# Raw expert weights as the high operand: the split into high and low halves moves from ScalarE copies to VectorE ANDs

## Chip, cores and metric
The kernel runs on one core of a Trainium2 chip. The metric is the device time of one execution in microseconds. Time before: 564.48 us, the median of three runs (564.39 to 565.3).

## What is computed
One layer on 16 sequences of 256 tokens with 256 features: retention attention with 8 heads and a layer norm, then a mixture of 8 experts (each token goes to one of them) beside a shared feed-forward part, and a second layer norm. The experts are what the change touches. Cut to that:

```python
E, H, I = (8, 256, 512)
logits = x @ router_w.T
top_vals, top_idx = jax.lax.top_k(logits, 1)
scores = sigmoid(scatter(top_vals))                       # -inf elsewhere
xr = x[None, :, :] * scores.T[:, :, None]
gate_up = jnp.einsum('eth,ehf->etf', xr, gate_up_proj)    # [8, 256, 1024]
gate, up = jnp.split(gate_up, 2, axis=-1)
routed = jnp.einsum('etf,efh->eth', up * jax.nn.silu(gate), down_proj)   # [8, 512, 256]
shared = jax.nn.silu(x @ shared_gate_w) * (x @ shared_up_w) @ shared_down_w
x = layernorm(x + shared + routed.sum(axis=0))
```

## The kernel before
Five engines run one hand-written instruction list each; semaphores order them, and each list is worked through strictly in order. PE (the trace's name) is TensorE, DVE is VectorE, ACT is ScalarE, POOL is GpSimd, SP issues most DMAs.

**The main loop** runs t from 0 to 9 (PAIRS + 1). Step t projects the pair of sequences t, does attention of pair a = t - 1 and the shared feed-forward part and routing of pair f = t - 2. Step 8 has no projection any more, step 9 only the feed-forward part of pair 7. In the trace, step 3 is about 92.9 to 135.95 us, step 4 runs to 178.85, step 8 is 306.9 to about 347, step 9 ends at 365.15.

**The slots** follow. The tokens are sorted by expert into 39 slots of 128. For each slot GpSimd gathers the rows (`gather`), TensorE transposes them, multiplies by the gate and up weights of the slot's expert (`slot_gate_up`, matmuls on line 1657 through the helper `three`), transposes and multiplies by the down weights (`slot_down`, line 2036). The first three gathers stand before GpSimd's slot loop, gather(s + 3) at the head of turn s.

**High and low halves.** Products are made of three passes in a reduced 32-bit format (fp32r): high x high, high x low, low x high (`PASSES`). So every weight matrix exists as a high half (the value rounded to the format) and a low half (value minus high half). For the gate and up weights of the eight experts (128x2048 each) ScalarE makes the high half by a copy (`expert_hi`, L781) into `w_gu_hi`, in this order: expert 6 in step 3; 0 to 4 in step 8; 5 and 7 in step 9. The low half is a subtraction over the raw value in `w_gu`: on VectorE for seven experts (`expert_lo`, L1253), on GpSimd for expert 5 (`expert_rest`, L978). The places in each engine's list are written out by hand. Before slot 0 TensorE waits for all eight:

```python
pe.wait_ge(sig.ew_lo, EXPERTS - 1)
pe.wait_ge(sig.ew_lo2, 1)
```

For the down weights (128x1024 each) there is no room for both halves of all experts on chip. In steps 3 to 6 (`PARTED`, two experts a step) SP loads one into `dn_raw`, ScalarE copies it to `dn_top` (`down_top`, L789), GpSimd subtracts into `dn_low` (`down_rest`, L991), and SP stores both halves to scratch in device memory. Later all high halves are loaded into `w_dn` (three from step 7's list, one from step 9's, four by ScalarE's queue after the loop), and the low half of a slot's expert is loaded for each slot.

**Neighbours that the prediction speaks of.** On VectorE: `x_lo` (L1116), `variance` (L1170), `group_norm` (L1182), `gated` (the gating product, L1192), `shared_product` (L1208), `shared_sum` (L1223), `output_sum` (L1233), `go_on` (a copy of 8 columns, L1390), `rows_lo` (L1560). On GpSimd: `group_rstd` (var_e on L947 and two power instructions on L952, released by `variance`), `residual` (L958). `last_products` is VectorE's list of step 9: four shared products with expert subtractions between them, after which come shared_sum and rows_lo(0).

## Time and profile before
| | |
|---|---|
| runs | 564.48, 565.3, 564.39 us |
| span of the profiled execution | 562.4 us; the page gives no other time for it, the median of the runs is 2.08 us longer |
| busy in the span | TensorE 544.5 us (97%), VectorE 415.9 (74%), ScalarE 234.3 (42%), GpSimd 322.6 (57%) |
| mean granted TensorE clock | 0.996 of 2.4 GHz |
| DMA | 83.55 MB, 149 GB/s over the span |

The span runs from the first to the last instruction of the core. Busy times overlap between engines, and a share over the whole span averages stages with different limits; a timeline row gives start and length in microseconds, the instruction, its tiles (out<-in), how often it stands there, and in brackets the idle time of the engine before it with what ended it.

### The profile page before, as it was taken

To read this page: it belongs to the slowest core of one execution; us is meant where nothing else is said; L and a number is where in the kernel's file an instruction comes from. 1 tells how busy PE (TensorE), PEld (TensorE's weight loads), DVE (VectorE), ACT (ScalarE), POOL (GpSimd) and SP (SyncE) were. 2 spreads that over 40 slices of the span, in tenths; PEclk is the share of its full clock that TensorE was granted. 3 is DMA by queue.
4 is the path that set the end of the run, shared out by engine and by line. 5 is a ranking of instruction groups with operands and counts; after the bars stand their busy time and mean duration, and the time that the engine had idled before them with its cause. 6 is when DMAs were issued, how large, how long until landed. Compare 5 with 4: busy or idle time off the path is not lost.

```text
span 562.4 us, 11872 instructions
## 1 busy us (share of the span) xinstructions
PE 544.5 (97%) x3884; PEld 455.6 (81%) x3884; DVE 415.9 (74%) x866; ACT 234.3 (42%) x415; POOL 322.6 (57%) x320
## 2 busy tenths in 40 slices
PE   7998999999999999999999899999999999999994
PEld 5776788778779779779778578888888888888884
DVE  4888977878877877977966687747866666666664
ACT  3435342555453463363353765133333333333331
POOL 0535493496395396296294283715786556666544
PEclk9999999999999999999999999999999999999998
DMA  7901206507608507705375524666667666656651
GB/s 258 310 11 39 76 2 62 128 25 136 216 4 172 201 2 154 222 0 173 119 272 193 197 101 113 219 228 183 197 161 200 194 188 196 184 196 198 196 180 37
DMA packets 46505, 83.55 MB, mean 149 GB/s; under 512 B 11584, under 2 KB 30528, under 8 KB 46432
## 3 DMA queue, kind: packets, MB, share of 16 engines
q1 hardware_dynamic: 38736, 64.27, 37.9%
q0 software_dynamic: 6048, 15.39, 10.3%
q10 hardware_dynamic: 1664, 3.15, 1.5%
q8 instruction: 33, 0.54, 0.4%
q14 instruction: 24, 0.20, 0.1%
HBM read 60.85 MB, written 22.34 MB: 148 GB/s over the span
## 4 chain that ended last, share of the span: by engine, by line
PE 89%; DVE 3%; POOL 2%; issue 2%; ACT 1%; POOLq 0%; ACTq 0%; DVEq 0%
PE duo L1657 51%; PE duo L2036 9%; PE duo L1881 6%; PE duo L1713 5%; PE duo L1735 4%; PE duo L2046 3%; PE duo L1885 2%; PE duo L1871 1%; PE duo L1817 1%; PE duo L1925 1%; PE duo L1775 1%; PE duo L1861 1%; PE duo L1793 1%; DVE sims L1149 1%; PE duo L1842 0%
## 5 line engine op out<-in xcount | busy, mean ns | idle before, releaser
L1657 PE MATMUL duo<-w_gu_hi,xsT 128*128 x320 | 107.7, 399 | 0.0
L1657 PE MATMUL duo<-x1T,wsgu 128*128 128x512 f32 x384 | 93.2, 395 | 0.0
L1657 PEld LDWEIGHTS duo<-x1T,wsgu 128*128 128x128 f32 x384 | 71.0, 188 | 15.5
L935 POOL TENSOR_TENSOR turned<-turned,swapped 128x1024 f32<-128x1024 f32 x16 | 38.5, 2423 | 65.4 <-DVE swapped L1140 65.4
L1076 POOL DMA_INDIRECT out_rows<-of,seat x39 | 39.4, 1011 | 56.0 <-DVE of L1614 53.8
L1657 PEld LDWEIGHTS duo<-w_gu_hi,xsT 128*128 128x128 f32 x320 | 59.7, 188 | 11.3
L1657 PE MATMUL duo<-w_gu,xsT 128*128 x160 | 61.5, 384 | 0.0
L1569 DVE SCALAR_TENSOR_TENSOR eh<-duo,seat,e_act 128x512 f32<-128x512 f32 x38 | 28.6, 751 | 40.1 <-PE duo L1657 36.4
L1149 DVE TENSOR_TENSOR sims<-duo,causal 128x512 f32<-128x512 f32 x64 | 41.2, 686 | 15.8 <-ACT sims L682 15.8
L1067 POOL DMA_INDIRECT xz<-xz_d,seat x39 | 44.9, 1152 | 9.2 <-issue 9.0
L682 ACT ACTIVATE sims<-duo 128x256 f32<-128x256 f32 x64 | 21.1, 382 | 69.3 <-PE duo L1713 69.0
L952 POOL TENSOR_TENSOR rstd<-var_e,minus_half 128x16 f32<-128x16 f32 x16 | 46.5, 2920 | 0.7
L2036 PE MATMUL duo<-w_dn,ehT 128*128 x152 | 46.0, 302 | 0.0
L908 ACT ACTIVATE ehT<-duo 128x512 fp32r<-128x512 f32 x38 | 22.8, 600 | 54.5 <-PE duo L2046 31.0
L1015 POOL DMA_INDIRECT seat_d<-stage,place_i x32 | 35.4, 1107 | 13.2 <-issue 11.6
L2036 PE MATMUL duo<-w_dn,ehT_lo 128*128 x152 | 42.8, 282 | 0.0
L2036 PE MATMUL duo<-dn_rest,ehT 128*128 128x256 f32 x152 | 42.6, 280 | 0.0
L901 ACT ACTIVATE e_act<-duo,seat 128x512 f32<-128x512 f32 x38 | 26.2, 690 | 32.1 <-PE duo L1657 29.8
L1657 PE MATMUL duo<-xT,wqk 128*128 128x512 f32 x144 | 39.0, 409 | 0.1
L1713 PEld LDWEIGHTS duo<-turned 32*128 32x128 f32 x512 | 26.1, 184 | 13.0 <-issue 9.0
L1713 PE MATMUL duo<-turned 32*128 32x128 f32 (+1 forms) x512 | 34.0, 349 | 1.6 <-DVE sims L1149 1.6
L1881 PE MATMUL duo<-wsd_s,hT_hi 128*128 128x256 f32 x192 | 35.2, 285 | 0.0
(192 smaller groups left out, 1279.5 us busy)
## 6 DMA issues: line engine op xcount, KB each, us to landing
dn_rest<-dn_lo_d SPq DMA_DIRECT2D x39, 512.0 KB
w_gu<-L_ffn_gate_up_proj SPq DMA_DIRECT2D x8, 1024.0 KB, 7.4
x_in<-x_t SPq DMA_DIRECT2D x8, 512.0 KB
x_res<-L_attn_x SPq DMA_DIRECT2D x8, 512.0 KB, 4.2
xz_d<-zs SPq DMA_DIRECT2D x8, 512.0 KB
dn_raw<-L_ffn_down_proj SPq DMA_DIRECT2D x8, 512.0 KB
dn_hi_d<-dn_top SPq DMA_DIRECT2D x8, 512.0 KB, 3.5
dn_lo_d<-dn_low SPq DMA_DIRECT2D x8, 512.0 KB
```

The lines of the kernel that those rows point to most:

```text
L901: nc.scalar.activation(e_act[:, :], duo[s % 2][:, 0, :], ACT.Silu, scale=f32(seat[:, s, :])[:, 2:3])\
L935: nc.gpsimd.tensor_tensor(turned[:, g, :, :], turned[:, g, :, :], swapped[:, g, :, :], ALU.add)\
L952: nc.gpsimd.tensor_tensor(rstd[:, half], var_e[:, half], minus_half[:, half], ALU.pow)\
L1015: pool.indirect_dma_start(seat_d, bass.IndirectOffsetOnAxis(ap=place_i[:, q:q + 1], axis=0), stage[:, q, :], None).then_inc(sig.scat, 16)
L1067: pool.indirect_dma_start(xz[:, s % ROWS, :], None, known, bass.IndirectOffsetOnAxis(ap=seat[:, s, 0:1], axis=0))\
L1076: pool.indirect_dma_start(out, bass.IndirectOffsetOnAxis(ap=seat[:, s, 1:2], axis=0), of[:, s % OUTS, :], None).then_inc(sig.out_done[s % ...
L1149: nc.vector.tensor_tensor(sims[:, j % 4, :, 0::2, :], src, mask, ALU.mult).then_inc(sig.s_diag, 1)
L1569: nc.vector.scalar_tensor_tensor(out=eh[:, :], in0=duo[s % 2][:, 1, :], scalar=f32(seat[:, s, :])[:, 2:3], in1=e_act[:, :], op0=ALU.mult, ...
L1657: last = mm(out_, left(a, k), right(b, k), start=start and k == 0 and n == 0, stop=stop and k == kt - 1 and n == len(PASSES) - 1)
L1713: last = mm(sim_duo(a, j)[:, i % 2, SEQ * kb:SEQ * kb + SEQ - P * kb], turned[rows, g, 1, key:key + P], turned[rows, g, 0, key:SEQ * (b + 1)],
L1881: last = mm(duo[2][:, q // 2, D * (q % 2):D * (q % 2 + 1)], left[:, q * P:(q + 1) * P], wsd_s[:, b, n, :], start=n + m == 0, stop=n == FT ...
L2036: last = mm(duo[2][:, 1, 0:D], halves[left][:, f, :], weights[right], start=f + n == 0, stop=f == FT - 1 and n == len(PASSES) - 1)
```

## The change
The raw fp32 weight is itself given to TensorE as the high operand (its bits read as fp32r), so the high halves need no place of their own. `w_gu` stays raw and `w_gu_hi` becomes `w_gu_lo`. VectorE writes the weight with its lowest 12 bits cleared (an integer AND with -4096) into `w_gu_lo` (`expert_cut`), and a subtraction in place, raw minus cut, makes the low half there. VectorE subtracts for experts 6, 0, 3 and 7, GpSimd for 1, 2, 5 and 4; its first two subtractions stand before the gathers, the last two between gather(2) and the slot loop. The down weights go the same way in `dn_low` (`down_cut` on VectorE, `down_rest` on GpSimd); only low halves are stored, and `w_dn` is loaded straight from the input. ScalarE has no part in the split any more. The diff without most of its unchanged lines:

```diff
 ROUTE = 13
+TOP_BITS = -4096
 PASSES = ((0, 0), (0, 1), (1, 0))
...
         seat_d = scratch("seat_d", [SEATS, SEAT], I32)
-        dn_hi_d = scratch("dn_hi_d", [EXPERTS * P, FT * D])
         dn_lo_d = scratch("dn_lo_d", [EXPERTS * P, FT * D])
...
             dn_raw = p_sb("dn_raw", [P, FT * D])
-            dn_top = p_sb("dn_top", [P, FT * D], F32R)
             dn_low = p_sb("dn_low", [P, FT * D], F32R)
+            dn_spare = p_sb("dn_spare", [P, FT * D])
...
         sb = tensors(ctx)
-        w_dn = sb("w_dn", [P, EXPERTS, FT, D], F32R)
+        w_dn = sb("w_dn", [P, EXPERTS, FT, D])
         w_gu = sb("w_gu", [P, EXPERTS, KT, 2 * FF])
-        w_gu_hi = sb("w_gu_hi", [P, EXPERTS, KT, 2 * FF], F32R)
+        w_gu_lo = sb("w_gu_lo", [P, EXPERTS, KT, 2 * FF], F32R)
...
             dn_raw_in = new("dn_raw_in")
-            dn_top_ok = new("dn_top_ok")
+            dn_cut_ok = new("dn_cut_ok")
             dn_low_ok = new("dn_low_ok")
-            dn_top_out = new("dn_top_out")
             dn_low_out = new("dn_low_out")
...
             ehT_low_ok = new("ehT_low_ok")
-            ew_hi = new("ew_hi")
+            ew_cut = new("ew_cut")
             ew_lo = new("ew_lo")
...
-                    sp.wait_ge(sig.dn_top_out, 16 * EXPERTS)
                     sp.wait_ge(sig.dn_low_out, 16 * EXPERTS)
...
                 sp.wait_ge(sig.dn_low_ok, e + 1)
-                sp.dma_start(dn_hi_d[rows, :], f32(dn_top[:, :])).then_inc(sig.dn_top_out, 16)
                 sp.dma_start(dn_lo_d[rows, :], f32(dn_low[:, :])).then_inc(sig.dn_low_out, 16)
...
             def down_in(e):
-                sp.dma_start(f32(w_dn[:, e, :, :]).rearrange("p f d -> p (f d)"), dn_hi_d[P * e:P * (e + 1), :])\
-                    .then_inc(sig.edn_in, 16)
+                sp.dma_start(w_dn[:, e, :, :], down[e].rearrange("(k p) n -> p k n", p=P)).then_inc(sig.edn_in, 16)
...
                                          scale=ln_r[:, q:q + 1]).then_inc(sig.x1_ok, 1)
-            def expert_hi(e):
-                act.wait_ge(sig.egu_in[e], 16)
-                if e < 2:
-                    act.wait_ge(sig.g_ps, KT * PAIRS)
-                    act.wait_ge(sig.xT_lo, KT * PAIRS)
-                elif e < 4:
-                    act.wait_ge(sig.av_ps, 4 * PAIRS)
-                elif e == 4:
-                    act.wait_ge(sig.var_ok, 2 * PAIRS)
-                elif e == 5:
-                    act.wait_ge(sig.o_ps, 2 * PAIRS)
-                elif e == 7:
-                    act.wait_ge(sig.o_ps, 2 * (PAIRS - 1))
-                nc.scalar.activation(w_gu_hi[:, e, :, :], w_gu[:, e, :, :], ACT.Copy).then_inc(sig.ew_hi, 1)
-            def down_top(e):
-                act.wait_ge(sig.dn_raw_in, 16 * (e + 1))
-                if e:
-                    act.wait_ge(sig.dn_top_out, 16 * e)
-                    act.wait_ge(sig.dn_low_ok, e)
-                nc.scalar.activation(dn_top[:, :], dn_raw[:, :], ACT.Copy).then_inc(sig.dn_top_ok, 1)
...
                         squared(a)
-                    if t == PAIRS:
-                        expert_hi(0)
                 if has(t):
...
                     logits_copy(f)
-                    if t == PAIRS:
-                        expert_hi(1)
-                    if t == PAIRS + 1:
-                        expert_hi(5)
-                        expert_hi(7)
                 if has(t + 1) and t != 1:
...
                     h_high(f, 0)
-                    if t in PARTED:
-                        down_top(PARTED[t][0])
                     shared_act(f, 1)
...
                         y_scaled(a)
-                        expert_hi(2)
                     shared_act(f, 2)
                     h_high(f, 2)
-                    if t == PAIRS:
-                        expert_hi(3)
                     shared_act(f, 3)
                     h_high(f, 3)
-                    if t == PAIRS:
-                        expert_hi(4)
                 if has(a) and t < PAIRS:
...
                         y_top(a)
-                    if t == 3:
-                        expert_hi(EXPERTS - 2)
-                    if t in PARTED and len(PARTED[t]) > 1:
-                        down_top(PARTED[t][1])
                     if t == 1:
...
             act.wait_ge(sig.gu_ps, 2 * FT * PAIRS)
-            act.wait_ge(sig.dn_top_out, 16 * EXPERTS)
             for e in range(4):
-                act.dma_start(f32(w_dn[:, e, :, :]).rearrange("p f d -> p (f d)"), dn_hi_d[P * e:P * (e + 1), :])\
-                    .then_inc(sig.edn_in, 16)
+                act.dma_start(w_dn[:, e, :, :], k_rows(down[e])).then_inc(sig.edn_in, 16)
...
-                pool.wait_ge(sig.ew_hi, n)
-                nc.gpsimd.tensor_tensor(w_gu[:, e, :, :].bitcast(F32R), w_gu[:, e, :, :], f32(w_gu_hi[:, e, :, :]),
+                pool.wait_ge(sig.ew_cut, n)
+                nc.gpsimd.tensor_tensor(w_gu_lo[:, e, :, :], w_gu[:, e, :, :], f32(w_gu_lo[:, e, :, :]),
                                         ALU.subtract).then_inc(sig.ew_lo2, 1)
...
-                pool.wait_ge(sig.dn_top_ok, e + 1)
-                if e:
-                    pool.wait_ge(sig.dn_low_out, 16 * e)
-                nc.gpsimd.tensor_tensor(dn_low[:, :], dn_raw[:, :], f32(dn_top[:, :]), ALU.subtract)\
+                pool.wait_ge(sig.dn_cut_ok, e + 1)
+                nc.gpsimd.tensor_tensor(dn_low[:, :], dn_raw[:, :], f32(dn_low[:, :]), ALU.subtract)\
                     .then_inc(sig.dn_low_ok, 1)
...
-            pool.wait_ge(sig.plan_ok, 2)
-            expert_rest(5, EXPERTS - 1)
+            expert_rest(1, 3)
+            expert_rest(2, 4)
...
             gather(2)
+            expert_rest(5, 6)
+            expert_rest(4, 7)
             for s in range(SLOTS + 2):
...
+            def expert_cut(e):
+                dve.wait_ge(sig.egu_in[e], 16)
+                if e < 2:
+                    dve.wait_ge(sig.g_ps, KT * PAIRS)
+                    dve.wait_ge(sig.xT_lo, KT * PAIRS)
+                elif e < 4:
+                    dve.wait_ge(sig.av_ps, 4 * PAIRS)
+                elif e == 4:
+                    dve.wait_ge(sig.var_ok, 2 * PAIRS)
+                elif e == 5:
+                    dve.wait_ge(sig.o_ps, 2 * PAIRS)
+                elif e == 7:
+                    dve.wait_ge(sig.o_ps, 2 * (PAIRS - 1))
+                nc.vector.tensor_scalar(w_gu_lo[:, e, :, :].bitcast(I32), w_gu[:, e, :, :].bitcast(I32), TOP_BITS, None,
+                                        ALU.bitwise_and).then_inc(sig.ew_cut, 1)
             def expert_lo(e, n):
...
-                dve.wait_ge(sig.ew_hi, n)
-                nc.vector.tensor_tensor(w_gu[:, e, :, :].bitcast(F32R), w_gu[:, e, :, :], f32(w_gu_hi[:, e, :, :]),
+                dve.wait_ge(sig.ew_cut, n)
+                nc.vector.tensor_tensor(w_gu_lo[:, e, :, :], w_gu[:, e, :, :], f32(w_gu_lo[:, e, :, :]),
                                         ALU.subtract).then_inc(sig.ew_lo, 1)
+            def down_cut(e):
+                dve.wait_ge(sig.dn_raw_in, 16 * (e + 1))
+                if e:
+                    dve.wait_ge(sig.dn_low_out, 16 * e)
+                nc.vector.tensor_scalar(dn_low[:, :].bitcast(I32), dn_raw[:, :].bitcast(I32), TOP_BITS, None,
+                                        ALU.bitwise_and).then_inc(sig.dn_cut_ok, 1)
...
                 shared_product(f, 1)
+                expert_cut(3)
                 expert_lo(3, 5)
-                for j in range(2, FT):
-                    shared_product(f, j)
-                expert_lo(4, 6)
+                shared_product(f, 2)
+                expert_cut(5)
+                expert_cut(4)
+                shared_product(f, 3)
+                expert_cut(7)
                 expert_lo(7, 8)
...
                 elif t == PAIRS:
+                    expert_cut(0)
                     x1_lo(f)
...
                     variance(a)
+                if t in PARTED:
+                    down_cut(PARTED[t][0])
                 if has(t + 1):
...
                         dve.wait_ge(sig.nmr_ok, PAIRS)
-                        expert_lo(1, 3)
+                        expert_cut(1)
                 if t == 1:
...
                     if t == 3:
+                        expert_cut(EXPERTS - 2)
                         expert_lo(EXPERTS - 2, 1)
...
                         x1_lo(a)
+                    if t in PARTED and len(PARTED[t]) > 1:
+                        down_cut(PARTED[t][1])
                     if t <= PAIRS:
...
                     if t == PAIRS:
-                        expert_lo(2, 4)
+                        expert_cut(2)
                 if t == 1:
...
-            gu_flat = (w_gu_hi[:, :, :, :].rearrange("p e k n -> p (e k n)"),
-                       w_gu[:, :, :, :].rearrange("p e k n -> p (e k n)").bitcast(F32R))
+            gu_flat = (w_gu[:, :, :, :].rearrange("p e k n -> p (e k n)").bitcast(F32R),
+                       w_gu_lo[:, :, :, :].rearrange("p e k n -> p (e k n)"))
             halves = (ehT, ehT_lo)
-            dn_flat = w_dn[:, :, :, :].rearrange("p e f n -> p (e f n)")
+            dn_flat = w_dn[:, :, :, :].rearrange("p e f n -> p (e f n)").bitcast(F32R)
...
-            pe.wait_ge(sig.ew_lo, EXPERTS - 1)
-            pe.wait_ge(sig.ew_lo2, 1)
+            pe.wait_ge(sig.ew_lo, 4)
+            pe.wait_ge(sig.ew_lo2, 4)
             last_e = this_e = next_e = None
...
                 last_e, this_e = this_e, first_e if s == 0 else next_e

```

## Rows read from the trace of the kernel before
**Rows 1.** Busy time by stretch (us, busy, instructions; PEclk; DMA share, GB/s).
```profile
306.90:332.75 25.85, 22.71 (x204) 16.58 (x205) 19.45 (x43) 16.41 (x27) 12.42 (x12) 1.00 0.53 189
332.75:365.15 32.40, 32.40 (x153) 27.15 (x154) 24.31 (x41) 14.54 (x18) 19.21 (x14) 1.00 0.45 140
365.15:553.40 188.25, 187.63 (x1171) 166.16 (x1170) 123.99 (x301) 65.04 (x117) 109.72 (x152) 1.00 0.62 188
```

**Rows 2.** TensorE's timeline, steps 8 and 9 (start, length; idle before).
```profile
332.75 3.69 PE L1925 MATMUL duo<-wo,yT 128*128 128x256 f32 x16 [0.64 <-DVE yT L1192]
...
357.86 5.34 PE L1885 MATMUL duo<-wsd,hT 128*128 128x256 f32 x24
```

**Rows 3.** Groups by form, whole span (busy us, mean ns).
```profile
L1560 DVE TENSOR_TENSOR xsT<-duo,xsT 128x256 fp32r<-128x256 f32 x39 | 16.2, 416 | 0.3
L1614 DVE TENSOR_SCALAR of<-of,mv,ln_r 128x256 f32<-128x256 f32 x39 | 15.9, 407 | 1.0 <-POOL ln_r L1086 1.0
...
L781 ACT ACTIVATE w_gu_hi<-w_gu 128x2048 fp32r<-128x2048 f32 x8 | 15.2, 1907 | 0.0
```

**Rows 4.** VectorE's timeline, step 8.
```profile
318.43 1.29 DVE L1162 TENSOR_TENSOR x1T<-duo,x1T 128x512 fp32r<-128x512 f32 x2 [2.29 <-ACT x1T L707]
319.74 1.28 DVE L1170 TENSOR_REDUCE var<-retT 128x16 f32<-128x512 f32 x2
322.04 2.29 DVE L1253 TENSOR_TENSOR w_gu<-w_gu,w_gu_hi 128x2048 fp32r<-128x2048 f32 x1 [1.01 <-ACT w_gu_hi L781]
...
328.53 1.14 DVE L1390 COPY start<-start 128x8 f32<-128x8 f32 x1
```

**Rows 5.** GpSimd's timeline, step 8.
```profile
321.11 0.30 POOL L947 TENSOR_SCALAR var_e<-var 128x32 f32<-128x32 f32 x1 [8.20 <-DVE var L1170]
321.50 5.80 POOL L952 TENSOR_TENSOR rstd<-var_e,minus_half 128x16 f32<-128x16 f32 x2
327.26 2.38 POOL L958 TENSOR_TENSOR x_res<-x_res,bias_o 128x1024 f32<-128x1024 f32 x1
```

**Rows 6.** ScalarE's timeline, step 4.
```profile
174.17 1.06 ACT L789 ACTIVATE dn_top<-dn_raw 128x1024 fp32r<-128x1024 f32 x1 [1.32 <-DMA dn_raw<-L_ffn_down_proj]
```

**Rows 7.** VectorE's timeline before slot 0.
```profile
353.22 2.68 DVE L1253 TENSOR_TENSOR w_gu<-w_gu,w_gu_hi 128x2048 fp32r<-128x2048 f32 x1
...
358.67 4.48 DVE L1253 TENSOR_TENSOR w_gu<-w_gu,w_gu_hi 128x2048 fp32r<-128x2048 f32 x2
```

**Rows 8.** GpSimd's timeline before slot 0.
```profile
349.12 4.64 POOL L978 TENSOR_TENSOR w_gu<-w_gu,w_gu_hi 128x2048 fp32r<-128x2048 f32 x1 [8.91 <-ACT w_gu_hi L781]
353.91 2.94 POOL L1067 DMA_INDIRECT xz<-xz_d,seat  x1 [0.15 <-issue]
...
358.44 0.95 POOL L1067 DMA_INDIRECT xz<-xz_d,seat  x1 [0.31 <-issue]
359.69 2.07 POOL L1067 DMA_INDIRECT xz<-xz_d,seat  x1 [0.30 <-issue]
```

**Rows 9.** VectorE's timeline, steps 3 and 4.
```profile
131.72 2.29 DVE L1253 TENSOR_TENSOR w_gu<-w_gu,w_gu_hi 128x2048 fp32r<-128x2048 f32 x1 [1.11 <-issue]
...
135.12 1.28 DVE L1233 TENSOR_TENSOR x_res<-duo,x_res 128x512 f32<-128x512 f32 x2
...
157.92 1.29 DVE L1116 TENSOR_TENSOR xT<-x_in,xT 128x512 fp32r<-128x512 f32 x2 [1.60 <-ACT xT L664]
...
175.15 0.69 DVE L1223 TENSOR_TENSOR zs<-duo,x 128x512 f32<-128x512 f32 x1 [0.98 <-PE duo L1881]
```

**Rows 10.** TensorE's timeline at the start of step 4.
```profile
135.95 1.63 PE L1657 MATMUL duo<-xT,wqk 128*128 128x512 f32 x6
```

**Rows 11.** Busy time by stretch, after the last matmul.
```profile
555.40:557.90 2.50, 0.00 (x0) 0.00 (x0) 1.59 (x5) 0.00 (x0) 1.10 (x4) 1.00 0.00 0
558.00:562.40 4.40, 0.00 (x0) 0.00 (x0) 0.07 (x1) 0.00 (x0) 1.75 (x2) 0.50 0.17 60
```

**Rows 12.** TensorE's timeline, opening.
```profile
1.46 5.02 PE L1938 MATMUL duo<-y 128*128 128x256 f32 x14 [1.46 <-DVE y L1413]
```

## Prediction
> **What bounds the kernel now.** I read the page's totals first (the table above): TensorE 97% busy, ScalarE 42%. An average says nothing about a stage, so next came the table by stretch [rows 1]. The reader is to see that TensorE works through all of 332.75 to 365.15 and 187.6 of the 188.3 us of the 39 slots, and that there is one stretch where it really idles: step 8, 306.9 to 332.75, with 22.71 of 25.85 us busy. So whatever makes TensorE start later after 332.75 is on the end in full, and a lighter ScalarE pays only if it closes part of those 3.1 us of idling. Third, TensorE's own timeline [rows 2]: the last wait before the slots is 0.64 us at 332.75, put down to VectorE's gating product; the last shared down projection begins at 357.86, and slot 0 follows it without a pause at 365.15. There is thus one gate to watch: the wait for all eight low halves in front of slot 0. Fourth come groups by form for the prices, and last the timelines of VectorE and GpSimd in step 8, before slot 0 and in steps 3 and 4, to see who is late.
>
> **What is removed.** ScalarE loses eight expert copies of 1.907 us, 15.3 us in all [rows 3], and eight of the down weights, half as large. It loses them beside TensorE work. The only visible idle of step 8 behind which ScalarE could stand is the 0.64 us at 332.75. That wait ends with the gating product on VectorE, which comes after go_on's tiny copy, and the copy lasts from 328.53 to 329.67 although it moves 8 elements: it ends with GpSimd's residual add (327.26 + 2.38 = 329.64) [rows 4, 5]. That residual comes after the two power instructions of 321.5 to 327.3, so step 8 hangs on GpSimd and the gain is 0 (bounds 0 and 0.64). Eight stores of 512 KB also go, and the eight loads of w_dn now come from the input in 1 KB pieces; no engine waits for them before slot 0's down projection, some 7 us after the gate. I cost them at nothing; without that cover the nearest row is ScalarE's wait of 1.32 us for a load of the same shape [rows 6].
>
> **Price of the AND.** No row shows a 128x2048 AND. Upper bound: VectorE's subtraction of that size, 2.29 us when nothing disturbs it [rows 4], and by the slope between it and the 128x256 form (0.416) 1.22 us for 128x1024. Lower bound: the same slope halved over a base of 0.16 us, 1.22 and 0.69 us, an estimate. I take the lower: the tensor-scalar instruction on 128x256, with two scalars read per partition, takes 0.407 us, less than the 0.416 of a subtraction of that size without any [rows 3]; at one element at a time the two scalars should cost something.
>
> The Trainium skill ("VectorE: DVE Perf Modes", the perf-mode tier table) gives an fp32 tensor-scalar of 2048 elements in SBUF 1.227 us; by it the sum stays as below, by the upper bound it becomes rival B.
>
> **What two engines do to each other.** At 353.22 a VectorE subtraction with two SBUF inputs takes 2.68 us instead of 2.29: GpSimd's subtraction was running until 353.76. The gather that GpSimd issues at 353.91 then takes 2.94 us and ends 0.95 us after VectorE is done at 355.90. The one at 359.69 takes 2.07 us and ends 0.85 us after the first of VectorE's two subtractions, which began at 358.67 [rows 7, 8]. The tiny copy above waited for GpSimd in the same way. I read this as: these VectorE instructions and GpSimd's exclude each other for a whole instruction, and who waits goes next when the other ends.
>
> The Trainium skill ("SBUF — State Buffer", who interferes with whom) says so: the shared port pair is an exclusive lock, taken by two-port VectorE instructions and, against GpSimd's reads, by those with two SBUF inputs. The trace agrees (2.68 against 2.29 us). By that rule the AND itself locks; without it the sum is rival A's.
>
> **Steps 3 to 6, down weights.** The first AND of a step stands behind the variance and ahead of x_lo, where VectorE idles 1.60 us in step 4 [rows 9]: 0.69 us is hidden. It may hold GpSimd's var_e back by half a microsecond; the chain behind that has about as much slack, so 0 (at most 0.1 us in each of four steps). The second stands between the two halves of shared_sum, where VectorE idles 0.98 us in step 4: 0 too; ScalarE waited for the load there until 174.17, and VectorE comes for it at that time [rows 6, 9]. In step 3 there is no such idle. There the expert's AND (130.6 to 131.8) just replaces the 1.11 us of idling in front of the subtraction at 131.72; but the down AND (0.69, less the 0.08 by which VectorE's instructions overlap) pushes output_sum by 0.61 us. Its first half ends at 136.42 instead of 135.81, and TensorE, whose next projection started at 135.95 right behind it, starts it **0.6 us** later [rows 9, 10]. At the upper price it is 1.0 + 1.1 = 2.1 us.
>
> **Step 8.** cut(0) falls into the 2.29 us that VectorE idles before x1_lo at 318.43. That has a consequence: expert 0's subtraction no longer waits for ScalarE until 322.04, but follows the variance, which ends at 321.02, at once [rows 4]. GpSimd's var_e, released by that variance, came at 321.11 [rows 5]. Now VectorE is first by about 0.1 us and holds the lock until 320.94 + 2.29 = 323.2; the power instructions, residual add, go_on, find_seats and gating product all move by 2.1 us. TensorE's output projection starts at 334.8 instead of 332.75: **+2.05 us** (bounds 0, if var_e wins, and 2.1). All later local times below are shifted by this, which I leave out of them.
>
> **The gate of slot 0.** GpSimd: before, one subtraction (4.64 us) [rows 8]; now four. rest(1) and rest(2) follow ANDs that stand where VectorE's subtractions 1 and 2 stood; I take them to end about when the one subtraction ended, 353.8, so that gathers 0 to 2 fill the gaps up to 359.3, as before. VectorE: cut(3) starts at 353.22, where lo(3) did [rows 7]; 1.22 for it, 2.29 for lo(3), 0.69 for product(2) and 1.22 for cut(5), less the overlaps, end at 358.4, cut(4) at 359.55, product(3) at 360.15; TensorE needs it after the first twelve matmuls of the down projection, 357.86 + 2.7 [rows 2], so in time. GpSimd gets the lock at 359.6 and keeps it through rest(5) to 364.2. Only then cut(7) runs, to 365.4; rest(4) has waited and goes next, to 370.0; lo(7) ends at 372.3, shared_sum 372.9, rows_lo(0) 373.3. Were lo(7) to go ahead of rest(4), rest(4) would end at 372.35. So slot 0's matmuls start at 372.35 to 373.3 instead of 365.15: **+7.2 to 8.15, I take 7.7 us**. Behind this wait stands all of the slot work of TensorE. gather(3), now behind both subtractions on GpSimd, is needed only two slots later.
>
> **The clock.** The granted clock is 1.00, that is 2.4 GHz, in the slots [rows 1]; after the last matmul, from 555.4 on, the clock still reads 1.00 until 557.9 and then 0.50, that is 1.2 GHz [rows 11]: an idle of 7 to 8 us is long enough for it to fall. What a restart costs is bounded by 0 and by slot 0's twelve gate-up matmuls (2.8 us) at half speed. Nearest row: the 14 opening matmuls took 5.02 us [rows 12], where 24 of the same form take 5.34 [rows 2], that is 3.1 for 14. I take the difference, rounded up, **2.0 us**. The Trainium skill ("TensorE: Matmul & The Clock Gate", the HAM clock gate) has an idle array fall to 1.2 GHz and start again from there; no row in the middle of this trace shows it.
>
> **Sum.** 0.6 + 2.05 + 7.7 + 2.0 = 12.35 us on a span of 562.4, so 574.75. The runs' median is 564.48, 2.08 us above the span; that stays around it: **576.8 us**, 2.2% slower. A change under 0.2% (1.1 us) cannot be told from none.
>
> **Rivals.**
> *A, no exclusion of that kind.* Then var_e is not held (0), and rest(5) and rest(4) run back to back from 358.6 to 368.0: +2.85, an idle too short to be sure of a slower clock. With 0.6: +3.45, 567.9 us. For it: GpSimd's power instructions ran beside VectorE's subtraction at 322.04, and the gather of 358.44 beside that of 358.67, without harm [rows 4, 5, 7, 8]; against it the rows of 2.68, 2.94 and 1.14 us [rows 4, 7, 8]. Chance 0.12.
> *B, the AND goes one element at a time.* Then it takes 2.29 us and VectorE is late: 2.1 in step 3, 2.05, product(3) at 363.2 (TensorE needs it at 360.6), slot 0 at 373.2: 2.1 + 2.05 + 8.05 + 2.0 = 14.2, 578.7 us. For it: no large two-at-a-time instruction in the trace; against it the 0.407 us row [rows 3]. Chance 0.13.
> *C, not slower.* The four GpSimd subtractions vanish beside TensorE, as the one did, and ScalarE's relief closes step 8's waits. It decides if rest(4) is done by 365.15. The AND of expert 5 cannot end before 358.4, so each of the two subtractions would have to take 3.35 us instead of 4.64. Then 562.4 - 0.64 + 0.6 is 562.4, that is 564.4 us, no change; if all 3.1 us of idling went, 562.0, faster. Chance 0.05 (0.02 of it faster).
> The forecast keeps 0.70. **Range** 570 to 580 us: it leaves out A and C and holds the forecast without clock loss (574.8), without step 8's loss (574.8), without both (572.7), and B with the full 2.8 us. Faster 0.02, same 0.03, slower 0.95.
>
> **What the next profile would show.** TensorE idle 7 to 8 us before the first matmul that reads w_gu, its PEclk under 1 just behind; four GpSimd subtractions of 4.6 us or more, the last ending after 370 (plus the shift); VectorE ANDs of 1.2 us, the one of expert 7 stretched to some 5; var_e of step 8 about 2 us late; step 3 longer by half a microsecond, steps 4 to 6 unchanged; ScalarE under 219 us and none the faster for it. I am wrong if GpSimd's subtractions run freely beside VectorE's (A), if the ANDs take 2.3 us (B), or if TensorE does not wait at the gate (C).

## The result and the profile after
The changed kernel takes 579.35 us (median of 4 runs, 578.92 to 579.54) beside 564.43 for the kernel before: ratio 1.0264, 95% interval 1.0253 to 1.0276, slower by 14.9 us. The forecast was 576.8 us, range 570 to 580. The profiled run took 579.54 us, its span is 577.6 (562.4 before). Line numbers are the changed kernel's own: L1215 `expert_cut`, L1221 and L930 the subtractions on VectorE and GpSimd, L1229 `down_cut`.

The page's totals and granted clock show the direction: TensorE was at 97% before, ScalarE at 42%; now it is 95% and 37%, and slice 27 of 40 (14.4 us each) has a lower clock.

```profile
PE 548.9 (95%) x3884; PEld 457.2 (79%) x3884; DVE 434.1 (75%) x879; ACT 212.6 (37%) x399; POOL 340.4 (59%) x323
...
PEclk9999999999999999999999999979999999999998
```

TensorE's timeline (start, length, idle before) says where. The marks to compare are the first projection after each of steps 3 to 6 (135.95, 178.78, 221.75, 264.72 before), the output projection of step 8 (332.75 in [rows 2]) and the start of slot 0 (365.15 in [rows 1]). The kernel before, with the last shared matmuls and slot 1's first:

```profile
178.78 1.66 PE L1657 MATMUL duo<-xT,wqk 128*128 128x512 f32 x6
...
221.75 1.66 PE L1657 MATMUL duo<-xT,wqk 128*128 128x512 f32 x6
...
264.72 1.66 PE L1657 MATMUL duo<-xT,wqk 128*128 128x512 f32 x6
...
363.25 1.89 PE L1885 MATMUL duo<-wsd,hT 128*128 128x256 f32 x8
...
369.16 0.50 PE L1657 MATMUL duo<-w_gu_hi,xsT 128*128 x1
```

The changed kernel:

```profile
137.19 1.63 PE L1642 MATMUL duo<-xT,wqk 128*128 128x512 f32 x6 [1.04 <-DVE x_res L1184]
...
180.21 1.66 PE L1642 MATMUL duo<-xT,wqk 128*128 128x512 f32 x6
...
223.42 1.66 PE L1642 MATMUL duo<-xT,wqk 128*128 128x512 f32 x6
...
266.64 1.66 PE L1642 MATMUL duo<-xT,wqk 128*128 128x512 f32 x6
...
336.63 3.69 PE L1910 MATMUL duo<-wo,yT 128*128 128x256 f32 x16 [0.82 <-DVE yT L1143]
...
367.22 1.89 PE L1870 MATMUL duo<-wsd,hT 128*128 128x256 f32 x8
377.37 0.79 PE L1642 MATMUL duo<-w_gu,xsT 128*128 x1 [8.26 <-DVE xsT L1545]
...
384.30 0.49 PE L1642 MATMUL duo<-w_gu,xsT 128*128 x1
```

The delay grows by 1.24 us in step 3, by 0.19, 0.24 and 0.25 in steps 4 to 6, by 1.96 up to the output projection, and the last shared matmul ends 3.97 us late (369.11 instead of 365.14). Then TensorE idles 8.26 us, where before it did not idle. From slot 0's first matmul to slot 1's first it then takes 6.93 us (377.37 to 384.30); in the run with a busy TensorE below that is 4.27, so 2.66 are lost. Sum: 1.24 + 0.68 + 1.96 + 0.09 + 8.26 + 2.66 = 14.9 of the 15.2 us that the span grew. The 0.3 that is missing is slot 0's first matmul, which before began at 364.80, ahead of the last shared one's end. Slot 1 begins 15.14 us late (384.30 instead of 369.16), so the slots behind it lose next to nothing.

The table by stretch shows the last term: PEclk falls while TensorE idles (0.55 from 373 to 375) and reads 0.50 in slot 0's matmuls.

```profile
371.00:373.00 2.00, 0.00 (x0) 0.00 (x0) 2.00 (x1) 0.00 (x0) 1.84 (x2) 1.00 0.55 176
373.00:375.00 2.00, 0.00 (x0) 0.00 (x0) 1.97 (x2) 0.00 (x0) 1.70 (x1) 0.55 0.00 1
...
381.00:383.00 2.00, 2.00 (x7) 1.39 (x5) 0.11 (x1) 0.02 (x1) 0.00 (x0) 0.50 0.71 242
383.00:385.00 2.00, 1.58 (x9) 1.04 (x8) 1.07 (x2) 0.98 (x2) 0.00 (x0) 0.89 0.07 7
```

VectorE's timeline, in the places of [rows 4, 7, 9], has the causes.

```profile
130.91 1.29 DVE L1215 TENSOR_SCALAR w_gu_lo<-w_gu 128x2048 int32<-128x2048 int32 x1
132.23 2.29 DVE L1221 TENSOR_TENSOR w_gu_lo<-w_gu,w_gu_lo 128x2048 fp32r<-128x2048 f32 x1
...
135.04 0.81 DVE L1229 TENSOR_SCALAR dn_low<-dn_raw 128x1024 int32<-128x1024 int32 x1
...
136.36 1.27 DVE L1184 TENSOR_TENSOR x_res<-duo,x_res 128x512 f32<-128x512 f32 x2
...
322.86 2.28 DVE L1221 TENSOR_TENSOR w_gu_lo<-w_gu,w_gu_lo 128x2048 fp32r<-128x2048 f32 x1
...
364.17 9.69 DVE L1215 TENSOR_SCALAR w_gu_lo<-w_gu 128x2048 int32<-128x2048 int32 x1
373.89 2.29 DVE L1221 TENSOR_TENSOR w_gu_lo<-w_gu,w_gu_lo 128x2048 fp32r<-128x2048 f32 x1
376.10 0.68 DVE L1174 TENSOR_TENSOR zs<-duo,x_last 128x512 f32<-128x512 f32 x1
376.70 0.41 DVE L1545 TENSOR_TENSOR xsT<-duo,xsT 128x256 fp32r<-128x256 f32 x1
```

And GpSimd's, beside [rows 5, 8]: var_e of step 3 and of step 8, then the subtractions of experts 5 and 4 back to back.

```profile
113.45 0.67 POOL L899 TENSOR_SCALAR var_e<-var 128x32 f32<-128x32 f32 x1 [0.81 <-DVE var L1121]
...
323.04 2.27 POOL L899 TENSOR_SCALAR var_e<-var 128x32 f32<-128x32 f32 x1 [8.21 <-DVE var L1121]
...
363.79 8.97 POOL L930 TENSOR_TENSOR w_gu_lo<-w_gu,w_gu_lo 128x2048 fp32r<-128x2048 f32 x2
```

The reader is to see the long AND of expert 7: an instruction of 1.2 us elsewhere takes 9.69 because it waits until both GpSimd subtractions (to 372.76) are through. After it come lo(7), a shared sum and the rows of slot 0, and only these release TensorE at 377.37.

### The profile page after: what moved, and what is told of

It reads as the page before. It is cut to its first block, busy times and chain, and to the rows that moved or that the text cites. A ratio compares the mean times of both kernels' runs of the same rounds, so it can differ in the third digit from the quotient of the medians.

```text
span 577.6 us, 11854 instructions
## 1 busy us (share of the span) xinstructions
PE 548.9 (95%) x3884; PEld 457.2 (79%) x3884; DVE 434.1 (75%) x879; ACT 212.6 (37%) x399; POOL 340.4 (59%) x323
## 4 chain that ended last, share of the span: by engine, by line
PE 75%; issue 8%; DVE 8%; POOL 6%; ACT 1%; POOLq 0%; DVEq 0%; ACTq 0%
PE duo L1642 44%; PE duo L2021 9%; PE duo L1866 4%; PE duo L1698 4%; PE duo L1720 3%; PE duo L2031 3%; DVE w_gu_lo L1215 2%; PE duo L1856 1%; POOL turned L887 1%; PE duo L1910 1%; PE duo L1870 1%; POOL rstd L904 1%; PE duo L1802 1%; PE duo L1760 1%; POOL seat_d L965 1%
## 5 line engine op out<-in xcount | busy, mean ns | idle before, releaser
L1642 PE MATMUL duo<-w_gu,xsT 128*128 x320 | 109.4, 405 | 8.3 <-DVE xsT L1545 8.3
L1642 PEld LDWEIGHTS duo<-w_gu,xsT 128*128 128x128 f32 x320 | 60.8, 191 | 20.5 <-issue 8.8
L1642 PE MATMUL duo<-w_gu_lo,xsT 128*128 x160 | 62.4, 390 | 0.0
```

What stands on the lines that cost most here:

```text
L1642: last = mm(out_, left(a, k), right(b, k), start=start and k == 0 and n == 0, stop=stop and k == kt - 1 and n == len(PASSES) - 1)
```

## Experiments
All runs are of the changed kernel with one edit, unless it says otherwise; ratios are to the kernel before, with 95% intervals.

**The gate: two subtractions taken from GpSimd.**
```diff
-            expert_rest(5, 6)
-            expert_rest(4, 7)
...
                 expert_cut(7)
+                expert_lo(5, 6)
+                expert_lo(4, 7)
                 expert_lo(7, 8)
...
-            pe.wait_ge(sig.ew_lo, 4)
-            pe.wait_ge(sig.ew_lo2, 4)
+            pe.wait_ge(sig.ew_lo, 6)
+            pe.wait_ge(sig.ew_lo2, 2)
```


> The changed kernel with the subtractions of experts 5 and 4 on VectorE instead of GpSimd. Mine (the gate of slot 0 is set by GpSimd's two subtractions, 8.97 us, through which VectorE's AND of expert 7 waits): VectorE then does AND 7 and three subtractions from 364.2, ends at 372.1, and TensorE starts slot 0 at about 373.1 with 4.0 us of idle instead of 8.26: 575.1 us, and down to 572.4 if the idle is too short for the clock to fall. The AND of expert 7 takes 1.24 us instead of 9.69. Rival one (the gate waits for the loads of experts 5, 4 and 7 and not for an engine): idle stays at 8 us, 579.3. Rival two (rival A of the prediction, engines do not exclude each other, the long AND is a wait for data): the AND stays long, 579.

574.98 us, ratio 1.0182 (1.0161 to 1.0202): 4.4 us back. VectorE's and TensorE's timelines of this run:

```profile
363.87 1.21 DVE L1213 TENSOR_SCALAR w_gu_lo<-w_gu 128x2048 int32<-128x2048 int32 x1
365.00 6.68 DVE L1219 TENSOR_TENSOR w_gu_lo<-w_gu,w_gu_lo 128x2048 fp32r<-128x2048 f32 x3
```
```profile
372.87 0.79 PE L1642 MATMUL duo<-w_gu,xsT 128*128 x1 [4.06 <-DVE xsT L1545]
...
379.65 0.50 PE L1642 MATMUL duo<-w_gu,xsT 128*128 x1
```
The AND is 1.21 us, the idle 4.06: the gate is the engines' time, not the loads. The clock still fell in these 4 us: slot 0 takes 6.78 us from first matmul to first matmul, so that term stays, 2.5 us.

**The clock: needless matmuls in the wait.**
```diff
+            for n in range(60):
+                mm(duo[0][:, 0, 0:P], ident[:, :], ident[:, :], start=True, stop=True)
             pe.wait_ge(sig.ew_lo, 4)
```


> The changed kernel with 60 needless 128x128 matmuls of ident in the wait ahead of slot 0, into a bank that slot 0 overwrites. Mine (the 2.7 us that slot 0's first twelve matmuls lose are the clock, which fell in the idle): the gate stays at 377.4, PEclk reads 1.00 throughout, the twelve matmuls take 2.8 us instead of 5.5: 576.65 us. Rival (they are slow because they share the memory with the loads and gathers that run at that time): they still take 5.5 us, 579.35.

581.93 us, ratio 1.0308 (1.029 to 1.0326), slower than expected: each of the 60 ran as two, they lasted 13.56 us and outlasted the gate by 4.7. The twelve matmuls behind them nevertheless ran at full speed: 4.25 us from slot 0's first matmul to slot 1's. So again with 32:

> As the run with 60 needless matmuls, with 32: each of them ran as two, so 60 lasted 13.56 us and outlasted the gate by 4.7 us; 32 last 7.2 us and end some 1.3 us before it. Clock theory: the gate at 377.3, the twelve matmuls 2.8 us, 576.65 us. Rival (contention with loads, of which there are fewer at 382 than at 377): the twelve matmuls take 5.5 us again, 579.35.

576.58 us, ratio 1.0219 (1.0205 to 1.0233): 2.8 us back. TensorE's timeline and the table by stretch:

```profile
368.64 7.31 PE L2083 MATMUL duo<-ident 128*128 128x128 f32 x64
377.09 0.49 PE L1642 MATMUL duo<-w_gu,xsT 128*128 x1 [1.14 <-DVE xsT L1545]
...
381.36 0.49 PE L1642 MATMUL duo<-w_gu,xsT 128*128 x1
```
```profile
377.00:380.00 3.00, 2.91 (x13) 2.37 (x14) 0.44 (x1) 0.69 (x1) 0.00 (x0) 1.00 0.75 233
```
The gate is where it was, the DMA share is no lower (0.75, and 0.68 in the same stretch of the changed kernel), and slot 0 takes 4.27 us at PEclk 1.00. The last term was the clock, not contention.

**Step 8: who begins first.** Three runs change only what stands between the variance and expert 0's subtraction: a wait for var_e; that wait and four one-column memsets; that wait and one reduction. The edit of the third, where `c_in` counts four early loads, that of `bias_o` among them:
```diff
                     variance(a)
+                    dve.wait_ge(sig.eps_ok, a + 1)
+                    dve.wait_ge(sig.c_in, 16 * 4)
+                    nc.vector.tensor_reduce(pace[:, 0:2], bias_o[:, :].rearrange("p (a b) -> p a b", a=2), X, ALU.add)
                     expert_lo(0, 2)
```


> The changed kernel with expert 0's subtraction on VectorE made to wait until GpSimd's var_e of step 8 is written. Mine (step 8 lost 1.95 us because the subtraction got ahead of var_e and held it for 2.27 us): var_e takes 0.3 us and all of step 8 behind it comes 1.9 us earlier, 577.4 us. Rival (the subtraction then runs into the power instructions or delays the group norm, so the loss moves): var_e short, but the output projection no earlier, 579.3.

579.0 us, ratio 1.0261 (1.0238 to 1.0285): nothing back. My theory fell: var_e is short now, but the power instructions take the loss over. GpSimd's timeline, with the subtraction beginning at 323.23:

```profile
322.89 0.30 POOL L899 TENSOR_SCALAR var_e<-var 128x32 f32<-128x32 f32 x1 [8.20 <-DVE var L1121]
323.27 7.90 POOL L904 TENSOR_TENSOR rstd<-var_e,minus_half 128x16 f32<-128x16 f32 x2
```


> As the run in which expert 0's subtraction waits for var_e, with four one-column memsets on VectorE between that wait and the subtraction. There the subtraction began at 323.23 and the two power instructions, due 0.04 us later, took 7.90 us instead of 5.80. Theory now (GpSimd's power instruction waits for a VectorE subtraction that has begun, but runs beside one that begins later): the power instructions begin first and take 5.8 us, the output projection comes 1.9 us earlier, 577.4 us. Rival (the power instructions are slowed by any subtraction beside them, or the loss moves to y): 579.0 as without the memsets.

579.18 us, ratio 1.0262 (1.0248 to 1.0276), and 7.93 us: the memsets took no time of their own, so this run told nothing new.

> As the run in which expert 0's subtraction waits for var_e, with one reduction over bias_o (one input in SBUF, some 0.3 us) between. The four memsets had put no time between (subtraction 322.96, power instructions 322.97, 7.93 us). Theory: with the power instruction begun first it is not held; the two take 5.8 us and the output projection comes 1.9 us earlier, 577.4 us. Rival one (any subtraction beside a power instruction holds it for its 2.1 us, whichever began first): still 7.9 us, 579.2. Rival two (the loss moves to y or to the subtraction's place on VectorE): 5.8 us, but 579.

577.02 us, ratio 1.0224 (1.021 to 1.0238): 2.3 us back. GpSimd, VectorE and TensorE in this run:

```profile
323.24 5.80 POOL L905 TENSOR_TENSOR rstd<-var_e,minus_half 128x16 f32<-128x16 f32 x2
```
```profile
323.53 2.28 DVE L1222 TENSOR_TENSOR w_gu_lo<-w_gu,w_gu_lo 128x2048 fp32r<-128x2048 f32 x1
```
```profile
334.50 3.69 PE L1914 MATMUL duo<-wo,yT 128*128 128x256 f32 x16 [0.69 <-DVE yT L1144]
```
The same two instructions side by side, but the power instruction began 0.29 us earlier: 5.80 us, and the output projection is at 334.50 instead of 336.63. Beginning 0.04 us later had cost it 2.1.

**The down weights alone undone.** ScalarE's `down_top`, `dn_top`, the stores of the high halves and the reloads come back as in the kernel before; `down_cut` goes.
```diff
+                nc.scalar.activation(dn_top[:, :], dn_raw[:, :], ACT.Copy).then_inc(sig.dn_top_ok, 1)
...
-                nc.vector.tensor_scalar(dn_low[:, :].bitcast(I32), dn_raw[:, :].bitcast(I32), TOP_BITS, None,
-                                        ALU.bitwise_and).then_inc(sig.dn_cut_ok, 1)
```


> The changed kernel with the down weights split as before (copy on ScalarE, both halves stored, w_dn loaded from the stored high halves), the gate-up weights as changed. Mine (the two ANDs of a step cost 1.1 us in step 3, of which 0.39 by holding var_e back, and 0.2 us in each of steps 4 to 6): 1.8 us comes back, 577.55 us, the projection of step 4 starts 0.1 us after that of the kernel before instead of 1.24. Rival one (step 3 lost its time to the AND of expert 6): about 0.6 us comes back, 578.7. Rival two (the stores and loads of the high halves that return cost as much as the ANDs): 579.3.

577.16 us, ratio 1.0222 (1.0204 to 1.0239): 2.2 us back. TensorE's projections behind steps 3 and 6 stand at or ahead of their places before (135.95 and 264.72):

```profile
135.85 1.62 PE L1651 MATMUL duo<-xT,wqk 128*128 128x512 f32 x6 [0.20 <-DVE x_res L1205]
...
264.51 1.66 PE L1651 MATMUL duo<-xT,wqk 128*128 128x512 f32 x6
```
The AND of expert 6, still in step 3, leaves 0.2 us of idle; the rest was the down weights' ANDs. At step 6's mark the run is 2.13 us ahead of the changed kernel (264.51 instead of 266.64), nearly all that came back.

**The raw operand alone.** The kernel before, with the raw weights as the high operand and the low half written over ScalarE's copy; the edit is the same in both subtractions.
```diff
-                nc.vector.tensor_tensor(w_gu[:, e, :, :].bitcast(F32R), w_gu[:, e, :, :], f32(w_gu_hi[:, e, :, :]),
+                nc.vector.tensor_tensor(w_gu_hi[:, e, :, :], w_gu[:, e, :, :], f32(w_gu_hi[:, e, :, :]),
...
-            gu_flat = (w_gu_hi[:, :, :, :].rearrange("p e k n -> p (e k n)"),
-                       w_gu[:, :, :, :].rearrange("p e k n -> p (e k n)").bitcast(F32R))
+            gu_flat = (w_gu[:, :, :, :].rearrange("p e k n -> p (e k n)").bitcast(F32R),
+                       w_gu_hi[:, :, :, :].rearrange("p e k n -> p (e k n)"))
```


> The kernel before with one part of the change alone: TensorE reads the raw gate-up weights as the high operand, and the subtraction writes over ScalarE's copy, in place. The copies stay on ScalarE, the subtractions where they were. Mine (the operand itself costs nothing; all of the loss comes from who makes the halves and when): 564.4 us, within 0.2%. Rival (raw operands or in-place subtraction cost time in the slots): each 1% on the 39 slots' 187 us gives 1.9 us, 566 or more.

564.1 us, ratio 1.0 (0.9991 to 1.0009; 11 runs). The operand and the subtraction in place cost nothing that 11 runs can tell.

**The order at the gate.** One run, no interval.
```diff
             expert_rest(5, 6)
+            gather(3)
             expert_rest(4, 7)
             for s in range(SLOTS + 2):
-                if is_slot(s + 3):
+                if s and is_slot(s + 3):
                     gather(s + 3)
```


> The changed kernel with GpSimd's fourth gather between its subtractions of experts 5 and 4 instead of behind both. Mine (locks add up, whatever their order): VectorE's AND of expert 7 gets in behind the first subtraction and takes 5.5 us instead of 9.69, but the last of the chain ends no earlier: the first matmul of slot 0 at 377 to 378, span 577 to 578.5. Rival (the order costs it: had the AND gone in between, as the prediction had it, lo(7) would overlap the second subtraction's wait): gate 1 to 2 us earlier.

578.72 us, span 576.0. VectorE, GpSimd and TensorE:

```profile
363.84 5.24 DVE L1216 TENSOR_SCALAR w_gu_lo<-w_gu 128x2048 int32<-128x2048 int32 x1
369.11 2.29 DVE L1222 TENSOR_TENSOR w_gu_lo<-w_gu,w_gu_lo 128x2048 fp32r<-128x2048 f32 x1
```
```profile
363.46 4.52 POOL L930 TENSOR_TENSOR w_gu_lo<-w_gu,w_gu_lo 128x2048 fp32r<-128x2048 f32 x1
368.14 1.78 POOL L1016 DMA_INDIRECT xz<-xz_d,seat  x1 [0.16 <-issue]
369.94 5.83 POOL L930 TENSOR_TENSOR w_gu_lo<-w_gu,w_gu_lo 128x2048 fp32r<-128x2048 f32 x1
```
```profile
375.97 0.79 PE L1643 MATMUL duo<-w_gu,xsT 128*128 x1 [7.20 <-POOL w_gu_lo L930]
```
Mine was right on the AND (5.24 us) and wrong on the gate: slot 0 begins at 375.97 and the idle is 7.20 instead of 8.26, as the rival had it. The locked times do add up in either order, but now GpSimd is the last, and the sum and slot 0's rows (0.9 us) run beside its subtraction instead of behind it.

**The same work, placed anew.** Three runs. The first moves expert 6 to step 7 (its subtraction to GpSimd), puts the first down AND of a step and expert 0's subtraction behind var_e and four memsets, ANDs 1 to 3 into step 8, and leaves GpSimd only experts 6 and 1.

> The changed kernel with the same work placed by what the other runs showed: expert 6's AND in step 7 and its subtraction on GpSimd behind that step's seats; the first down AND of a step and expert 0's subtraction behind var_e and four small memsets; ANDs 1, 2 and 3 in step 8; only experts 6 and 1 subtracted on GpSimd, the rest on VectorE. Mine: steps 3 to 6 give back 2.0 us, step 8 gives back 1.9, the gate's idle falls from 8.26 to between 0 and 1 us and the clock does not fall (2.7): 564.4 to 565.5 us, the time before, not under it. Rival (VectorE has no room for 6 ANDs and 5 subtractions there): the gate keeps 2 to 3 us, 567 to 568, or 570 with the clock.

571.38 us, ratio 1.0119 (1.0104 to 1.0134). Steps 3 to 6 are back at their old places and the gate is gone: TensorE goes from the shared projection into slot 0 at 372.16 without idling. But the power instructions are held as before (7.93), and there is a new wait. VectorE, GpSimd and TensorE:

```profile
343.04 4.39 DVE L1275 CAST slots_f<-slots_i 128x8 f32<-128x8 int32 x1
```
```profile
342.84 4.55 POOL L931 TENSOR_TENSOR w_gu_lo<-w_gu,w_gu_lo 128x2048 fp32r<-128x2048 f32 x1
```
```profile
351.14 1.89 PE L1810 MATMUL duo<-x1T,wr 128*16 128x512 f32 x4 [2.96 <-DVE x1T L1113]
```
A cast of 8 columns, 0.17 us elsewhere, takes 4.39 because it waits for GpSimd, and behind it wait x1_lo and TensorE. The clock fell twice on the way: after waits of 0.33 and 1.22 us in step 8 twelve matmuls took 4.21 us (3.00 in the changed kernel), and after the 2.96 us PEclk read 0.50 from 351 to 353.

> The run with the work placed anew, mended where its profile showed two waits (power instructions of step 8 7.93 us; the plan's one 8-element cast 4.39 us, because GpSimd's subtraction of expert 1 ran, and so x1_lo 3 us late): expert 0's AND ahead of the last masked similarities and its subtraction on GpSimd ahead of var_e, expert 1's subtraction on GpSimd only when the plan is made, go_on's copy ahead of GpSimd's residual add. Mine: 2 us back in step 8, 3 us behind it, 0.6 from go_on's copy: 564 to 566 us, the time before within 0.3%. Rival (what TensorE no longer waits for there, VectorE then lacks at the gate): 567 to 569.

569.07 us, ratio 1.0084 (1.007 to 1.0097), short of mine: I had put the AND of expert 1 where GpSimd's subtraction of expert 0 runs, 4.58 us with x1_lo behind it (2.9 us of TensorE), AND 2 beside a power instruction of the seats and AND 3 beside one of the last norm. GpSimd, where AND 2 runs from 334.82 to 336.04:

```profile
333.81 2.27 POOL L958 TENSOR_TENSOR stage<-powed,minus_one 128x4 f32<-128x4 f32 x1
```

It takes 1.04 us in the changed kernel. Begun 1.01 us ahead of the AND, it still ended with it; so did the norm's (342.46 to 344.47, AND 3 from 343.21 to 344.43).

> The last placing with its two new waits mended. There expert 1's AND waited 3.4 us for GpSimd's subtraction of expert 0 with x1_lo behind it (2.9 us of TensorE), and the ANDs of experts 2 and 3 held GpSimd's one-column power instructions, so that the last norm came 1.2 us late. Now ANDs 1 and 3 stand behind the variance and a small reduction, where VectorE waits for TensorE, AND 2 behind the plan and the norm's scales, and GpSimd's subtraction of expert 1 behind AND 2. Mine (TensorE then waits 0.4 us in step 8 and 0.2 to 0.7 at the gate more than in the kernel before): 564.4 to 565.5 us, the time before within 0.2%. Rival (VectorE is full from step 8 to the gate, and any place for these ANDs delays something): 567 or more.

The edit is against the run before it; the first line puts GpSimd's subtraction of expert 1 behind AND 2.
```diff
-            expert_rest(1, 3)
+            expert_rest(1, 5)
...
-                    expert_cut(1)
                     x1_lo(f)
                     variance(a)
+                    dve.wait_ge(sig.eps_ok, a + 1)
+                    dve.wait_ge(sig.c_in, 16 * 4)
+                    nc.vector.tensor_reduce(pace[:, 0:2], bias_o[:, :].rearrange("p (a b) -> p a b", a=2), X, ALU.add)
+                    expert_cut(1)
+                    expert_cut(3)
...
-                        expert_cut(2)
...
                         plan_early()
-                        expert_cut(3)
+                        dve.wait_ge(sig.nmr_ok, PAIRS)
+                        expert_cut(2)
...
-                        expert_lo(2, 4)
-                        expert_lo(3, 5)
+                        expert_lo(2, 5)
+                        expert_lo(3, 4)
```
564.9 us (11 runs), ratio 1.0017 (1.0007 to 1.0026): the whole split without ScalarE, 14.5 us faster than the changed kernel and within 0.3% of the kernel before. TensorE's waits (total, times, longest) and its timeline at the gate:

```profile
PE duo L1735 <- DVE sims L1103: 2.1, 2, 1.2
```
```profile
360.54 2.86 PE L1885 MATMUL duo<-wsd,hT 128*128 128x256 f32 x12 [0.29 <-DVE hT L1162]
...
365.26 0.49 PE L1657 MATMUL duo<-w_gu,xsT 128*128 x1
```
No gate is left (slot 0 starts at 365.26 without a wait); the similarities wait 2.1 us in all (1.7 before), because expert 0's AND stands in front of the last, and 0.29 us go ahead of the last shared projection.

## Why the prediction was right, and where its terms were off
The direction, the order of the terms and most of the mechanism held; the forecast was 2.6 us too low, and the time is near the upper end of the range. Errors did not cancel: every term that was off by more than 0.1 us was too low.

- **Removed work, 0.** Held as far as the runs tell. Without ScalarE's copies TensorE still waits for the gating product in step 8, 0.82 us (0.64 before). The raw operand with the copies takes 564.1 us, the last placing without them 564.9. No run takes away ScalarE's work and nothing else, so the 0 itself is not shown. The stores and reloads that went are worth little: with them back the run was faster by 2.2 us, for the ANDs that went.
- **Price of the AND, 1.22 and 0.69 us.** Held: 1.21 to 1.29 and 0.68 where nothing disturbs it. Rival B is out.
- **Step 3, 0.6 us.** The mechanism was right and half of it was missing: 1.24. The down AND delays output_sum by 0.73, 0.12 of them because it is that much longer than elsewhere (0.81 us, while GpSimd's store of the seats runs); expert 6's AND is 0.12 slower than the idle that it fills; and the first down AND holds var_e (0.67 instead of 0.30), which arrives at y_rest as 0.39 (129.63 instead of 129.24).
- **Steps 4 to 6, 0.** A step that failed: "the chain behind that has about as much slack, so 0 (at most 0.1 us in each of four steps)". It was 0.19, 0.24 and 0.25. Holding var_e back was seen (its median is 0.67 us instead of 0.30), the slack behind it overrated; the run without down ANDs has none of the loss.
- **Step 8, 2.05 us.** It was 1.96, by the mechanism named: the subtraction is first by 0.18 us and var_e waits. What I had not seen is that the power instruction behind var_e can be held just so; in the kernel before it had begun 0.54 us ahead of the subtraction [rows 4, 5]. The "for it" of rival A (power instructions ran beside the subtraction without harm) thus told only who came first. The Trainium skill ("SBUF — State Buffer", who interferes with whom) says that the order of issue decides who blocks; the pair of runs with 7.90 and 5.80 us agrees. The two power instructions of the second placing that began ahead of an AND and still ended with it do not.
- **The gate, 7.7 us.** It was 8.26, just above the term's upper bound of 8.15. The step "who waits goes next when the other ends" failed for the AND of expert 7, which was to be stretched to some 5 us and took 9.69: GpSimd's second subtraction followed the first at once, and the AND, lo(7), the sum and the rows came behind both. The size came out near all the same, because with lo(7) last the engines' times add up alike in either order; the 7.7 was a middle between lo(7) last and the second subtraction last. With a gather between, the AND went in after the first subtraction, lo(7) followed it while GpSimd was at the gather, and the idle was 7.20, the lower bound of the term.
- **The clock, 2.0 us.** It was 2.66, near the upper bound: all of slot 0's gate-up matmuls ran at 0.50, that is 1.2 GHz. The Trainium skill ("TensorE: Matmul & The Clock Gate", the HAM clock gate) has an idle array fall to that clock; the run with a busy TensorE, at 1.00 throughout, agrees.
- **Rivals.** A is out by the instructions that waited (9.69, 4.39 and 7.90 us). C is out for this placing; the last run shows that it was a matter of placing.

## What to carry to other kernels
When work moves from ScalarE to VectorE or GpSimd, don't add up its durations alone: list every GpSimd instruction that may run beside each large VectorE one, and what stands behind whichever of the two waits. A cheap instruction (an AND of 1.2 us, a cast of 8 columns) can cost as much as the longest one of the other engine, and a reorder by 0.3 us can give it back. An idle of 4 us on TensorE costs its own length and then the clock, here 2.5 us more.

## What was not expected of the hardware
- An engine that keeps its instructions coming can keep the other one out: the AND took 9.69 us because it waited through two GpSimd subtractions back to back (8.97 us). Why two GpSimd instructions in a row leave no gap, where a gather between them does, stays open.
- A power instruction of 16 columns is held for a whole VectorE subtraction when it begins 0.04 us after it (7.90 us for two), and not at all when it begins 0.29 us before (5.80).
- Beginning first does not always protect: beside an AND, power instructions of 4 columns that had begun 1.01 and 0.75 us earlier took 2.27 and 2.01 us instead of 1.04 and ended with it. Why an AND can do this and the subtraction did not stays open; the power instruction of 2.9 us beside the subtraction would have ended after it anyway.
- Memsets of one column took no time in VectorE's order: three of them and the subtraction behind them show the same start, 322.96.
- TensorE's clock had fallen to 0.50 after an idle of 4.06 us as well as after 8.26, and slot 0 paid nearly the same for both (6.78 and 6.93 us instead of 4.27). In two profiled runs it fell in step 8 after waits of about 0.3 and 1.22 us (the memsets, PEclk 0.55; the first placing, 0.51), and the twelve matmuls behind them took 4.29 and 4.21 us instead of 3.00. In the run with the wait for var_e alone, with 0.25 and 1.22 at the same place, it stayed at 1.00.
